# A third buffer of down values, another order in the tail of the third LayerNorm stage, idle TensorE products, and output products and clears at other pairs

## The reference

```
x = x + L0_xattn(layernorm(x), ctx)        # FFT correlation, top 4 rolls
x = x + L0_ffn(layernorm(x))               # frequency-domain matrix, bias
x = x + L1_xattn(layernorm(x), ctx)        # sampling
x = x + L1_ffn(layernorm(x))               # fake-quantised gate, up, down

# L1_xattn, for each token, head (16) and point (4):
v    = ctx @ w_value + b_value
off  = query @ w_off + b_off;  attw = softmax(query @ w_attw + b_attw)
ix, iy = places from off;  x0 = floor(ix);  fx = ix - x0
sampled = v[x0] * (1 - fx) * m0 * hy + v[x0 + 1] * fx * m1 * hy
out  = sum over points of sampled * attw, then @ w_out + b_out

# L1_ffn: every activation is rounded to a grid whose step is the tensor's peak / 32767:
x = qdq(x); up = qdq(x @ Wu.T); gate = qdq(x @ Wg.T)
gate = qdq(gate * u16(sigmoid(gate))); o = qdq(gate * up); out = o @ Wd.T
```

## Time and profile before

| What | Value |
|---|---|
| runs of the kernel | 1006.37, 1020.7 and 1021.2 us, median 1020.7 |
| the profiled execution | 1004.41 us, of which the span is 1002.6 us |
| busy: PE, DVE, ACT, POOL | 838.5, 684.9, 539.4, 306.0 us |
| mean granted TensorE clock | 0.932 of full speed |
| sampling | starts at 410.14 us; last pair's hat is done at 629.9 us |
| one quad of sampling in its steady part | 27.30 us |
| hidden products (o) | first at 856.4, last at 905.9 us |
| down products | 914.72 to 999.5 us |

### The profile page before, as it was taken

The page is one execution under the profiler, slowest core; times in us unless marked ns, Lnnn a source line. Parts: engine busy times, 40 slices in busy tenths (PEclk is TensorE's granted clock), DMA queues, the critical chain, the costliest instruction groups (busy, mean ns, idle before and its releaser), DMA issues.

```text
span 1002.6 us, 12939 instructions
## 1 busy us (share of the span) xinstructions
PE 838.5 (84%) x4501; PEld 539.6 (54%) x4501; DVE 684.9 (68%) x1237; ACT 539.4 (54%) x1009; POOL 306.0 (31%) x236
## 2 busy tenths in 40 slices
PE   4999998799999998788888899599998994005998
PEld 3776675577777886244444444344443441004887
DVE  2567767866775676579888888735534999895333
ACT  2444434455334665666666666134428995982432
POOL 2100000566110222587777778200010431000000
PEclk9999999799999999599999999799998997556999
DMA  9800000010000000000000000000002436710111
GB/s 290 256 1 1 1 1 1 0 55 0 2 11 1 1 1 1 0 2 1 1 1 1 2 1 2 1 0 1 0 1 84 168 146 275 262 71 11 53 52 53
DMA packets 23446, 45.41 MB, mean 45 GB/s; under 512 B 2323, under 2 KB 18646, under 8 KB 22230
## 3 DMA queue, kind: packets, MB, share of 16 engines
q1 hardware_dynamic: 21776, 43.08, 12.1%
q10 hardware_dynamic: 1606, 1.52, 0.5%
HBM read 27.80 MB, written 16.78 MB: 44 GB/s over the span
## 4 chain that ended last, share of the span: by engine, by line
PE 60%; DVE 20%; POOL 8%; ACT 6%; issue 5%; ACTq 1%; DMA 0%; DVEq 0%; POOLq 0%
PE pair L1313 8%; PE pair L1272 8%; POOL hat L596 5%; PE pair L967 5%; PE pair L1194 4%; PE pair L1075 3%; PE pair L1102 3%; PE pair L1208 3%; PE pair L971 3%; DVE peak L1758 2%; DVE wide L1753 2%; DVE peak L1743 2%; DVE wide L1781 2%; PE pair L1012 2%; PE pair L1104 2%
## 5 line engine op out<-in xcount | busy, mean ns | idle before, releaser
L596 POOL TENSOR_TENSOR hat<-hat 128x1024 f32<-128x1024 f32 x62 | 145.6, 2360 | 45.1 <-DVE hat L1619 44.4
L1178 PE MATMUL pair<-rows,sel 32*128 32x512 bf16 x256 | 75.4, 397 | 23.1 <-ACT down_b L816 17.3
L1619 DVE SCALAR_TENSOR_TENSOR hat<-pair,down_a 128x1024 f32<-128x1024 f32 x64 | 78.1, 1220 | 21.8 <-PE pair L1170 19.7
L1297 PE MATMUL pair<-xqs,wuT 128*128 128x512 f32 x192 | 85.9, 610 | 4.8 <-ACT up_stage L861 4.8
L816 ACT ACTIVATE down_b<-pair 128x512 f32<-128x512 f32 x128 | 69.4, 595 | 37.0 <-PE pair L1178 32.1
L816 ACT ACTIVATE down_a<-pair 128x512 f32<-128x512 f32 x128 | 69.5, 595 | 33.5 <-PE pair L1178 24.0
L1313 PE MATMUL pair<-wdT,hid 128*128 128x256 f32 x384 | 84.8, 384 | 2.9 <-DVE hid L1800 2.9
L1619 DVE SCALAR_TENSOR_TENSOR hat<-pair,down_b 128x1024 f32<-128x1024 f32 x64 | 78.0, 1219 | 11.9 <-PE pair L1170 11.7
L1272 PE MATMUL pair<-xqs,wgT 128*128 128x512 f32 x192 | 85.1, 601 | 0.0
L1313 PEld LDWEIGHTS pair<-wdT,hid 128*128 128x128 f32 x384 | 74.1, 193 | 13.5 <-DVE hid L1800 3.2
L513 POOL TENSOR_TENSOR rstd<-lnt,half 128x8 f32<-128x8 f32 (+2 forms) x15 | 26.5, 1769 | 167.5 <-DVE lnt L1354 167.5
(11 more groups left out here) (208 smaller groups left out, 1880.8 us busy)
## 6 DMA issues: line engine op xcount, KB each, us to landing
up_far<-up_stage SPq DMA_DIRECT2D x24, 512.0 KB, 2.6
ups<-up_far SPq DMA_DIRECT2D x8, 1536.0 KB, 6.7
x_sb<-in_x_dram SPq DMA_DIRECT2D x8, 512.0 KB, 8.2
c_sb<-in_ctx_dram SPq DMA_DIRECT2D x8, 512.0 KB, 9.0
out_dram<-x_sb SPq DMA_DIRECT2D x16, 256.0 KB, 2.1
four<-in_c_four_dram SPq DMA_DIRECT2D x1, 1280.0 KB, 5.7
deq<-in_L_ffn_w_gate_dram SPq DMA_DIRECT2D x1, 768.0 KB, 6.8
deq<-in_L_ffn_w_up_dram SPq DMA_DIRECT2D x1, 768.0 KB, 8.5
```

The source lines that it names most:

```text
L596: nc.gpsimd.tensor_tensor(hat[:, n % RING, :], hat[:, (n - 2) % RING, :], hat[:, n % RING, :], ALU.add).then_inc(summed, 1)
L1178: mm(bank[6 + i], sel[g:g + 32, pp, 1, :], rows[g:g + 32, q, c * 2 + a, :], start=True, stop=True).then_inc(down_mm, 1)
L1297: last = mm(bank[2 + oc], wuT[:, c, oc * 128:(oc + 1) * 128], xqs[:, t % 2, c, :], start=(c == 0), stop=(c == DC - 1))
L1619: V.scalar_tensor_tensor(hat[:, n % RING, :], pair[n % 2][:].rearrange("p i t -> p (i t)"), 0.0, down[n % 2][:].rearrange("p i t -> p (i t ...
```

## The change

A third buffer `down_c` lets ACT's Relu of pair n wait for the hat of pair n - 3. In ACT's tick the exponent now stands first, ahead of the kept rows, and `keep_v63(0)` and `(1)` move from S5 + B + 1 to S5 + B + 3, behind the steps of that tick. On TensorE `turn_parts` stands ahead of `values63`, and at S5 + B + 6 six idle products stand ahead of `turn_w63` and ten behind it; six more follow the loop. In the sampling the clears are at t = 2 and 12, `edge(q + 1)` is behind the seventh sum, and the output product is cut into single sequences at t = 4, 6, 8 and 10. After the last output product stand 36 idle products. Ahead of `spread_peak(4)`, and once 14 of the 16 hidden products are done, stand 16 idle f32 products of 128 x 128 by 512.

```diff
-        down = [down_a, down_b]
+        down = [down_a, down_b, sb("down_c", [128, 2, QUAD * L], F32, sample)]
 # GpSimd
-                    if j == 7 and q < NQ - 1:
+                    if j == 6 and q < NQ - 1:
                         edge(q + 1)
 # ScalarE, tick loop
-                if t == S5 + B + 1:
+                for tick, step in ((2, exponent), (10, keep_rows), (7, second_part), (5, first_part)):
+                    if group_at(t, tick) is not None:
+                        step(group_at(t, tick))
+                if t == S5 + B + 3:
                     keep_v63(0)
                     keep_v63(1)
-                for tick, step in ((10, keep_rows), (7, second_part), (2, exponent), (5, first_part)):
-                    if group_at(t, tick) is not None:
-                        step(group_at(t, tick))
 # ScalarE, sampling
-                    if n >= 2:
-                        act.wait_ge(hat_done, n - 1)
-                    nc.scalar.activation(down[n % 2][:, i, :], bank[6 + i], ACT.Relu).then_inc(down_done, 1)
+                    if n >= 3:
+                        act.wait_ge(hat_done, n - 2)
+                    nc.scalar.activation(down[n % 3][:, i, :], bank[6 + i], ACT.Relu).then_inc(down_done, 1)
 # TensorE
+            def keep_busy(n, place):
+                for _ in range(n):
+                    mm(place, idn16[:], rows[:, 0, 0, :], start=True, stop=True)
+
+                if t == S5 + B + 6:
+                    pe.wait_ge(v_kept, B)
+                    pe.wait_ge(off_kept, B)
+                    keep_busy(6, bank[3])
+                    turn_w63()
+                    keep_busy(10, bank[3])
+                if group_at(t, 9) is not None:
+                    turn_parts(group_at(t, 9))
                 if t == S5 + B + 1:
                     for p in range(NQ // 2):
                         values63(p)
-                if t == S5 + B + 6:
-                    turn_w63()
-                if group_at(t, 9) is not None:
-                    turn_parts(group_at(t, 9))
+            keep_busy(6, bank[3])
...
-            def project_att(q, i):
-                pe.wait_ge(attT_copied, 2 * q + 2)
-                if i:
-                    pe.wait_ge(x3_done, 2 * q + 1)
-                mm(bank[5] ..., ones3, bias3 ..., start=True, stop=False)
-                for b in range(2):
-                    for c in range(DC):
-                        last = mm(...)
-                last.then_inc(out_mm, 1)
+            def project_att(q, i, b):
+                if b == 0:
+                    pe.wait_ge(attT_copied, 2 * q + 2)
+                    if i:
+                        pe.wait_ge(x3_done, 2 * q + 1)
+                    mm(bank[5] ..., ones3, bias3 ..., start=True, stop=False)
+                for c in range(DC):
+                    last = mm(...)
+                if b:
+                    last.then_inc(out_mm, 1)
...
-                if t in (4, 13):
-                    clear_att(q, t // 8)
+                if t in (2, 12):
+                    clear_att(q, t // 12)
                 if n >= 5 and n % 2 == 1:
                     take((n - 5) // 2)
-                if q and t in (6, 10):
-                    project_att(q - 1, t // 10)
+                if q and t in (4, 6, 8, 10):
+                    project_att(q - 1, t // 8, t // 2 % 2)
...
-            project_att(NQ - 1, 0)
-            project_att(NQ - 1, 1)
+            for b in range(2):
+                project_att(NQ - 1, 0, b)
+            for b in range(2):
+                project_att(NQ - 1, 1, b)
+            pe.wait_ge(hat_done, PAIRS)
+            keep_busy(36, bank[3])
...
+            def keep_rest():
+                for _ in range(16):
+                    mm(bank[3], wdT[:, 0, 0:128], wdT[:].rearrange("p c o -> p (c o)")[:, 0:512], start=True, stop=True)
...
             pe.wait_ge(up_kept, UPS)
+            pe.wait_ge(o_done, HALVES - 2)
+            keep_rest()
             spread_peak(4)
```

More of the change, by code:

```diff
@@ L1197, in take @@
                 last.then_inc(taken, 1)
-            def project_att(q, i):
-                pe.wait_ge(attT_copied, 2 * q + 2)
-                if i:
-                    pe.wait_ge(x3_done, 2 * q + 1)
-                mm(bank[5][:].rearrange("p (b d) -> p b d", b=2), ones3,
-                   bias3[:, BAT["bout"]:BAT["bout"] + D].unsqueeze(1).broadcast_to([3, 2, D]), start=True, stop=False)
-                for b in range(2):
-                    for c in range(DC):
-                        last = mm(bank[5][:, b * D:(b + 1) * D], attT[:, c, (2 * i + b) * L:(2 * i + b + 1) * L], wout_sb[:, c, :],
-                                  start=False, stop=(b == 1 and c == DC - 1))
-                last.then_inc(out_mm, 1)
+            def project_att(q, i, b):
[3 more added lines that the diff above has]
+                        pe.wait_ge(x3_done, 2 * q + 1)
+                    mm(bank[5][:].rearrange("p (b d) -> p b d", b=2), ones3,
+                       bias3[:, BAT["bout"]:BAT["bout"] + D].unsqueeze(1).broadcast_to([3, 2, D]), start=True, stop=False)
+                for c in range(DC):
+                    last = mm(bank[5][:, b * D:(b + 1) * D], attT[:, c, (2 * i + b) * L:(2 * i + b + 1) * L], wout_sb[:, c, :],
+                              start=False, stop=(b == 1 and c == DC - 1))
+                if b:
+                    last.then_inc(out_mm, 1)
             def clear_att(q, c):
@@ L1619, in sample_dve @@
                 V.scalar_tensor_tensor(hat[:, n % RING, :], pair[n % 2][:].rearrange("p i t -> p (i t)"), 0.0,
-                                       down[n % 2][:].rearrange("p i t -> p (i t)"), ALU.max, ALU.min).then_inc(hat_done, 1)
+                                       down[n % 3][:].rearrange("p i t -> p (i t)"), ALU.max, ALU.min).then_inc(hat_done, 1)
                 q, t = n // TURN, n % TURN
```

## The result

| | kernel before | kernel after |
|---|---|---|
| median of the runs, us | 1020.81 (1006.37 to 1021.2) | 1026.74 (1024.58 to 1033.63) |
| ratio of times, to the shorter runs of the kernel before | | 1.023 [1.0199, 1.0258] |
| the profiled execution's time; its span | 1004.4; 1002.6 | 1024.69; 1022.9 |
| mean granted clock | 0.932 | 0.923 |

The runs of the kernel before lie at about 1005 and at about 1021 us, and the ratio compares with the shorter ones, so that the change costs 6 us against the median of the kernel before and 20 to 23 against those. I had forecast 1005.

What follows compares the result with a forecast made beforehand. No single engine was taken to bound the kernel (TensorE 60% of the chain, DVE 20%). Terms 0.4 - 4.7 - 2.2 + 0.2 + 5.0 = -1.3; 1006.4 - 1.3 gave 1005 us, range 996 to 1021.

Steps and rivals of the forecast that it cites:

- Clears and single output products: Sampling quads: with moved clears, split output products and earlier edge, 27.4 against 27.30 us, seven times: +0.4; ends +8, -27.1.
- Clock at the start of sampling: First sampling products: TensorE enters at 2.4 GHz instead of rising 13 us in, -2.2 us; ends 0 and -3.
- Rival 4: Sampling turn: the late take costs its full 1.16 us in seven quads, +8, so 1013; chance 0.07.
- Third buffer: Sampling: removes ACT's 13.5 us of waiting for DVE but gains 0; ends 0 and -27.1.
- Tail: End of the tick loop: reordered turns and idle products start sampling at 405.4, -4.7 us; ends -5.7 and +2.
- The 0.95 of the collision: Tail: DVE's small operation beside POOL's residual took 1.24 us, its neighbour 0.29; the 0.95 was left in.
- 36 idle products: After the last output product: they last 7.9 us, first spread 1.8 late, +0.2; ends -0.3, +1.9, +9.7 at 1.2 GHz.
- 16 idle f32 products: Ahead of the last spread: they last 16.0 us, spread 5.8 late, half of 1.6 won back, +5.0; ends +3.4, +6.4.
- The spread of the runs: Median: two runs 15 us longer than the profiled one; forecast 1005 if idle products take that away, 1019 otherwise.
- The candidate: Start of sampling: one more quad with TensorE at 1.2 GHz, 13.7 us, would explain the 15 us between runs.
- Rival 2: Sampling becomes DVE-bound; half of DVE's 27.1 us of waits goes, 13 less: 992; chance 0.08.
- Rival 3: Ahead of the last spread: idle f32 products at 1.2 GHz take 27.4 us, 1015 or 1032 from the median; chance 0.07.

Runs made afterwards that it cites:

- Experiment 9: The kernel before with only POOL's edge moved ahead of the eighth sum; 1040.04 us, ratio 1.0335 to the kernel before.
- Experiment 3: The changed kernel plus idle products in TensorE's two gaps, four before the clear of t = 2, three before the take of t = 3; 1015.04 us, ratio 1.0093.
- experiment 1: The changed kernel with the edge back behind the eighth sum and the first clear back at t = 4; 998.54 us, ratio 0.9935.
- Experiment 8: The changed kernel with the edge behind the sixth sum, plus two idle products in each of pairs 1 to 5 of the first quad; 991.75 us, ratio 0.975.
- experiment 6: The kernel before with only the new tail order and its 22 idle products; 1001.0 us, ratio 0.9857.
- experiment 2: The changed kernel with the edge one place earlier, behind the sixth sum; 1004.72 us, ratio 0.9978.
- experiment 5: The kernel before with only the third down buffer added; ratio 1.0016, ten runs from 1004.96 to 1021.94 us.
- experiment 10: Experiment 8 with the output products in pairs again, at t = 6 and 10; 996.01 us, ratio 0.9918 to the kernel before.
- experiment 12: Experiment 8 with 27 and 10 idle products in place of the 36 and 16; 986.42 us, ratio 0.9831 to the kernel before.

## Why the prediction was wrong

**The step that failed** is "Clears and single output products", +0.4, with its ends of +8 and -27.1. It came to +15.5. Its working holds: the quads that kept their clock took 27.41 and 27.43 against the forecast 27.4 (hat 14 to hat 7 14.95 against 15.0, hat 7 to hat 14 12.46 against 12.4), POOL's list ran as drawn, and the take was 1.06 us late where I had 1.16. What it leaves out is TensorE's clock in that turn. I had POOL's lateness, its gap on TensorE and even the price of a quad at 1.2 GHz in the same text (13.7 us, in the part on the median), and never brought them together; in "Clock at the start of sampling" I wrote that no gap over 1.5 us is left, as if shorter ones were safe. Experiment 9 shows one of 1.01 us, added to the turn of the kernel before, lowering the clock for some 7 us and costing 3.4 us per quad. Experiment 3 shows that with the same lateness and the gaps filled the quad is 0.3 longer than before. Whether it is the idle time that lowers the clock, or the little work around it, the runs do not part: the idle products of experiment 3 change both, and the kernel before has three waits of 0.5 us in the same stretch and keeps its clock. Rival 4 had the right place and the wrong price: it multiplied the lateness, 1.16, and its end of +8 is half of what came.

**Clock at the start of sampling**, -2.2, failed in the same way: +2.2. TensorE did enter at 2.4 GHz, and fell at 412.8, 4.9 us in, during the first clear; ahead of it stand the first pairs, where it has only products with 32 rows and waits for ACT's Relus between them. It was low for 20.5 us. In experiment 1, low for 6.8, the stretch took 2.0 less than before, near the forecast. Experiment 8, with ten idle products among these pairs, holds the clock in its profile. Why experiment 6 loses it for 6.8 us there and experiment 2 for 44, no run shows.

**Third buffer**, 0: right alone (experiment 5). **Tail**, -4.7: right, -5.2. The 0.95 of the collision was rightly left in.

**36 idle products**, +0.2: +1.0, inside its ends. They took 7.72 us against my 7.9. **16 idle f32 products**, +5.0: +3.6, inside 3.4 to 6.4. They lasted 15.7 (forecast 16.0) with 3.5 us of low clock at their start, and the 1.6 us of the down products was all won, where I had counted half. With 16 of them in experiment 10 (6.0 us of low clock) and with 10 in experiment 12 it was lost, so both ends of that coin were seen.

**The spread of the runs.** The candidate was right in kind: experiment 5 shows a low clock until 465.9 in an execution of 1021.9, worth 12.3 us, and the mean clocks on record part the two groups of the kernel before in the same way. Its price of 13.7 counts a take as 0.96 dearer, where rows 6 and 8 have 1.92 - 1.07 = 0.85, so 12.8. The hope built on it, that the change would take it away, held in the four runs of the tail alone (experiment 6). With the rest of the change beside it the clock was low for 20 (the changed kernel), 24 (experiment 3) and 44 us (experiment 2) at the same place.

**Rival 2**, a DVE-bound sampling at 992, had a chance of 0.08. The sampling comes close to it once POOL is out of the way: experiment 8 has 1.5 us less per quad than before (9.7 in seven, where the rival had 13), and DVE's wait for up values is 1.9 per quad instead of 3.8. That its median of 991.75 is the rival's number is luck, since the tail is in it too. **Rival 3** did not happen, and its point, a low stretch of over 7.2 us in the 16 products, was not reached (3.5 us in the changed kernel, 6.0 at most, in experiment 10). The sum was off in one term by 15 and in another by 4.4; the stage of +3.0 ahead of the change is neither's.

## What to carry to other kernels

Price a wait on TensorE twice: once as lost time, once as what the clock will do after it. Where the clock was lost, a gap of 1 us cost 3.4 (experiment 9). So put a helper engine's side work (here POOL's edge, 1.7 us) into that engine's own wait, never ahead of a result that TensorE is about to need; that one place in a list cost 21 us in six quads here. Idle products pay where the clock falls without them and where they end before the awaited value: 7 per quad took the quads from 30.7 to 27.6, 27 ahead of the first spread won 0.4, ten ahead of the last won nothing, and 16 there, which end after the value is ready, cost 3.4. And when runs of one kernel fall into two groups, read the granted clock of each run before comparing medians.

## What the runs showed of the hardware that was not expected

- TensorE's clock fell behind a wait of 1.01 us in experiment 9, the only one in the turn that the kernel before lacks, and it stayed at 1.2 GHz for about 7 us there, and for 7 to 10 us behind the waits of the changed kernel. The Trainium skill, TensorE: Matmul & The Clock Gate (HAM oscillation — how this bites in real kernels), tells of a loop whose waits for DMA put the clock back down in each round. The round is the same here; the wait is for another engine, and is short.
- In one execution of the changed kernel the same turn lost the clock in five quads of seven, in three of them already behind the 0.77 us for the clear, and kept it in two, one of which had both waits (0.77 and 0.66) in full.
- The time at 1.2 GHz at the start of the sampling is anything from none (experiment 8, with ten idle products there) over 6.8 (411.7 to 418.5, experiment 6) and 44 (experiment 2) to 61 us (404.5 to 465.9, experiment 5), with almost the same work on TensorE. It stayed low through 48 us (416 to 464) in which TensorE was busy for 45.7. It makes up most of the 15 us by which runs of one kernel differ.
